# A two-layer graph kernel on one core: complete blocks multiplied once for both layers with 512 columns, and five rounds of early sums for the first tiles

## The reference

```
# layer 0
deg = sum(adj, axis=1);  x1 = adj @ x / deg
x = layernorm(x + concat([x1, x]) @ weight + bias)
# layer 1
h = x @ W.T;  e = h@a1 (row) + h@a2 (column), -inf where adj == 0
x = layernorm(x + softmax(e, axis=1) @ h)
```

## Time and profile before

| | us |
|---|---|
| three runs: lowest, median, highest | 1010.03, 1012.83, 1012.96 |
| the profiled execution, its own time | 1011.9 |
| its span in the profile | 1010.2 |
| PE busy | 970.8 (96%) |
| DVE busy | 732.5 (73%) |
| ACT busy | 601.8 (60%) |
| first pass (tiles 0 to 63) ends at about | 750 |

### The profile page before, as it was taken

The page is one execution under the profiler, slowest core; times in us unless marked ns, Lnnn a source line. Parts: engine busy times, 40 slices in busy tenths (PEclk is TensorE's granted clock), DMA queues, the critical chain, the costliest instruction groups (busy, mean ns, idle before and its releaser), DMA issues.

```text
span 1010.2 us, 22065 instructions
## 1 busy us (share of the span) xinstructions
PE 970.8 (96%) x8727; PEld 866.9 (86%) x8727; DVE 732.5 (73%) x1791; ACT 601.8 (60%) x604; POOL 277.1 (27%) x275
## 2 busy tenths in 40 slices
PE   6899889999999998999999999999999999999996
PEld 6899767888988897888898888888888888888885
DVE  3698887888877786778777676666654986677674
ACT  3988898888878887988868676767421000000000
POOL 4345544333435433434333333332000000000000
PEclk9999989999998999999999999999999999999999
DMA  9999999999999999999999999999421022222101
GB/s 283 394 420 420 421 420 421 419 421 421 421 421 417 420 418 422 415 419 414 410 392 362 420 344 349 341 350 311 159 77 71 22 84 86 90 90 89 34 24 34
DMA packets 50490, 301.70 MB, mean 299 GB/s; under 512 B 6608, under 2 KB 7888, under 8 KB 17360
## 3 DMA queue, kind: packets, MB, share of 16 engines
q0 software_dynamic: 37344, 270.03, 66.9%
q1 hardware_dynamic: 12336, 29.47, 8.7%
q10 hardware_dynamic: 704, 0.75, 0.3%
HBM read 286.46 MB, written 13.76 MB: 297 GB/s over the span
## 4 chain that ended last, share of the span: by engine, by line
PE 61%; DMA 27%; ACT 7%; issue 3%; DVE 2%; POOL 0%; ACTq 0%; DVEq 0%
PE ps_agg L403 33%; DMA adj_in<-in_adj_dram,chunk 26%; PE ps_part L403 22%; ACT edges L585 5%; PE ps_y L403 4%; PE ps_h L752 1%; ACT parts L576 1%; PE ps_h L707 0%; DMA x_all<-in_x_dram 0%; DVE parts L911 0%; PE ps_x1T L745 0%; POOL adj_in L1399 0%; DVE packed L963 0%; DVE edgesT L948 0%; PE ps_y L707 0%
## 5 line engine op out<-in xcount | busy, mean ns | idle before, releaser
L403 PE MATMUL ps_agg<-parts,edgesT 128*128 128x255 f16 (+1 forms) x5240 | 592.3, 274 | 20.3 <-DVE edgesT L948 18.9
L403 PEld LDWEIGHTS ps_agg<-parts,edgesT 128*128 128x128 fp8e4 x5240 | 514.2, 98 | 85.7 <-DVE edgesT L948 24.2
L585 ACT ACTIVATE edges<-adj_in 128x2048 fp8e4<-128x2048 int32 x256 | 481.2, 1905 | 62.8 <-DMA adj_in<-in_adj_dram,chunk 61.2
L1399 POOL DMA_INDIRECT adj_in<-in_adj_dram,chunk x256 | 272.2, 1063 | 430.4 <-ACT edges L585 419.7
L948 DVE STREAM_TRANSPOSE edgesT<-edges 128x512 uint32<-128x512 uint32 x256 | 167.1, 691 | 60.2 <-ACT edges L585 59.6
L403 PE MATMUL ps_part<-parts,edgesT 128*128 128x256 f16 x1664 | 190.2, 273 | 0.3 <-DVE parts L1050 0.3
L403 PEld LDWEIGHTS ps_part<-parts,edgesT 128*128 128x128 fp8e4 x1664 | 162.8, 98 | 18.8 <-DVE parts L1050 0.5
L652 ACT ACTIVATE std<-mean_var,eps 128x1 f32<-128x1 f32 x64 | 18.9, 295 | 226.4 <-DVE mean_var L1224 226.4
L963 DVE SCALAR_TENSOR_TENSOR packed<-edgesT,packed 128x2048 uint32<-128x2048 uint32 x48 | 109.6, 2283 | 1.2 <-DVE packed L959 0.5
L403 PE MATMUL ps_part<-parts,packed 128*128 128x256 f16 x772 | 87.2, 273 | 0.0
L403 PEld LDWEIGHTS ps_part<-parts,packed 128*128 128x128 fp8e4 x772 | 75.6, 98 | 8.7
(11 more groups left out here) (125 smaller groups left out, 655.3 us busy)
## 6 DMA issues: line engine op xcount, KB each, us to landing
adj_in<-in_adj_dram,chunk POOLq DMA_INDIRECT x256
adj_in<-partial_sums SPq DMA_DIRECT2D x16, 256.0 KB, 5.7
out_dram<-edges SPq DMA_DIRECT2D x60, 64.0 KB, 3.3
partial_sums<-partial SPq DMA_DIRECT2D x13, 256.0 KB
packed_adj<-parts SPq DMA_DIRECT2D x2, 1024.0 KB
adj_in<-packed_adj SPq DMA_DIRECT2D x2, 832.0 KB, 5.1
x_all<-in_x_dram POOLq DMA_DIRECT2D x6, 256.0 KB, 13.1
x_all<-in_x_dram SPq DMA_DIRECT2D x6, 256.0 KB, 14.8
```

The source lines that it names most:

```text
L403: done = eng.matmul(bank[:, 0:cols], rows[:, n // BYTES, n % BYTES, :], moving[:, n, :], start=(n == first), stop=(n == last))
L585: act.activation(edges[:, r // 2, r % 2, :], adj_in[:, m % SLOTS, :], ACT.Copy, scale=EDGE[t % GROUP], saturate=False).then_inc(s_conv, 1)
L1399: pool.indirect_dma_start(adj_in[:, m % SLOTS, :], None, adj_chunks, bass.IndirectOffsetOnAxis(chunk[:, 0:1], 0), element_offset=first_row ...
```

## The change

- `parts0` and `parts1` become one tile `rows01`, in which a block has 512 fp16 columns: 256 of the first layer, then 256 of the second.
- For tiles of group g >= 3, `first_layer(t)` issues block 0 with all 512 columns, then the blocks that are not complete (from `done` = 4(g - 1) on) with 255. `hidden(t - 3)` follows, and then `both_layers(t)`: it waits for `s_lo1 >= g - 1` and issues blocks 1 to done - 1 with 512 columns. Both sums lie in the one bank `ps_agg[t % 2]`; `s_agg` is raised at the end of `both_layers`, so that `degree(t)` and `keep_partial(t)` both wait for that. `ps_part` is no longer used in the first pass.
- The caught tiles come in five rounds, two tiles at a time in four of them: groups 0 and 1 get 4 groups of blocks, group 2 gets 3 (before 2, 3 and 4). That is 176 matmuls, 32 more than before, and 32 fewer behind the first pass. Their sums alternate between two banks, and two more stores go to `part_dram`; the loads of these and two additions on DVE come behind the first pass.
- Words and sums that lie in late blocks are now strided by block, so the stores of these (`store_caught`, and `store_words` of pairs 0 and 1) have runs of 512 B in place of 2 KB and 8 KB. The stores of pairs 1 and 0 come one group later.

```diff
-    CATCH = 12
-    CAUGHT = [2, 3, 4]
+    ROUNDS = [(0, 0, 2, 12, 2), (1, 0, 2, 14, 2), (2, 0, 3, 16, 1), (0, 2, 2, 20, 2), (1, 2, 2, 22, 2)]
...
-        parts0 = sb("parts0", [P, NBLK, 2 * F], fp16)
-        parts1 = sb("parts1", [P, NBLK, XCOLS], fp16)
+        rows01 = sb("rows01", [P, NBLK * BOTH + 2 * NBLK], fp16)
+        both = rows01[:, 0:NBLK * BOTH].rearrange("p (n f) -> p n f", f=BOTH)
+        parts0 = both[:, :, 0:2 * F]
+        parts1 = both[:, :, 2 * F:BOTH]
...
             for g in range(GROUPS - 1):
+                for k in range(len(ROUNDS)):
+                    if GROUP * g < kept_at(k) < GROUP * (g + 1):
+                        store_caught(k)
...
-                    if g == KEEP_UNTIL[n] - 1:
+                    if g == KEEP_UNTIL[n]:
                         store_words(n)
...
+            def bank_ready(t):
                 pe.wait_ge(s_tr, NQ * (t + 1))
                 wait(pe, s_z, t - 1)
+                if inline(t - 2):
+                    pe.wait_ge(s_partk, t - 2 - EARLY + 1)
...
+            def first_layer(t):
+                words, done = by_bands(edgesT[:, t % 2, :]), GROUP * bands_of(t // GROUP)
+                bank_ready(t)
+                if not inline(t):
...
+                else:
+                    contract(pe, ps_agg[t % 2], words, both, [0], 0, done - 1)
+                    contract(pe, ps_agg[t % 2], words, parts0[:, :, 0:LO + KEPT_F], range(done, NBLK), 0, done - 1)
+
+            def both_layers(t):
+                done = GROUP * bands_of(t // GROUP)
+                pe.wait_ge(s_lo1, bands_of(t // GROUP))
+                contract(pe, ps_agg[t % 2], by_bands(edgesT[:, t % 2, :]), both, range(1, done), 0, done - 1)\
+                    .then_inc(s_agg, 1)
...
-            def second_layer_inline(t):
...
-                pe.wait_ge(s_lo1, bands)
-                wait(pe, s_partk, t - EARLY)
-                contract(pe, ps_part, edgesT[:, t % 2, :], weighted_rows, range(0, bands * GROUP), 0, bands * GROUP - 1)\
-                    .then_inc(s_part, 1)
...
             def keep_partial(t):
                 g, c = t // GROUP, t % GROUP
-                dve.wait_ge(s_part, t - EARLY + 1)
+                dve.wait_ge(s_agg, t + 1)
...
-                if catching(t):
-                    unpack_caught(t - CATCH)
-                if catching(t - 1):
-                    keep_caught(t - 1 - CATCH)
                 if t // GROUP in odd_groups and t % GROUP == GROUP - 1:
                     check(t // GROUP, 0)
...
                 if joins:
                     check(t // GROUP - 1, 1)
                     join(t // (2 * GROUP) - 1)
+                for i, k, c in caught_at(t):
+                    unpack_caught(i, k, c)
+                for i, k, c in caught_at(t - 1):
+                    keep_caught(i, k)
...
+                for i, k in enumerate(SECOND):
+                    if c == 0 and g == ROUNDS[k][0]:
+                        dve.wait_ge(s_partld2[i], 16)
+                        dve.tensor_tensor(part_in[:, s, :], part_in[:, s, :], part_in[:, 5 + i, :], ALU.add)\
+                            .then_inc(s_pjoin, 1)
```

More of the change, by code:

```diff
@@ L53, in bass_two_graph_layers, with caught_at @@
     EARLY = FIRST_INLINE * GROUP
-    CATCH = 12
-    CAUGHT = [2, 3, 4]
-    CTILES = GROUP * len(CAUGHT)
-    CWORDS = P * max(CAUGHT)
+    ROUNDS = [(0, 0, 2, 12, 2), (1, 0, 2, 14, 2), (2, 0, 3, 16, 1), (0, 2, 2, 20, 2), (1, 2, 2, 22, 2)]
+    CAUGHT = [max(first + bands for g, first, bands, at, by in ROUNDS if g == k) for k in range(FIRST_INLINE)]
+    CBANDS = max(bands for g, first, bands, at, by in ROUNDS)
+    SECOND = [k for k in range(len(ROUNDS)) if ROUNDS[k][1] > 0]
+    def caught_at(t):
+        return [(GROUP * k + c, k, c) for k, (g, first, bands, at, by) in enumerate(ROUNDS) for c in range(GROUP)
+                if t == at + c // by]
     def bands_of(g):
@@ L328, in bass_two_graph_layers @@
         s_partld = [sem(f"partial_landed{s}") for s in range(5)]
+        s_partld2 = [sem(f"partial_of_second_round_landed{g}") for g in range(len(SECOND))]
+        s_pjoin = sem("rounds_added")
         s_unp = sem("unpacked")
@@ L383, in on, with round_home @@
             return 0 <= t - lag < TILES
[L385 to L386 removed]
+        def round_home(k):
+            return GROUPS + SECOND.index(k) if k in SECOND else ROUNDS[k][0]
         def inline(t):
@@ L752, in hidden, with caught @@
                 pe.matmul(ps_h[:, 0:HCOLS], x1T[:, :], w1_cols[:, :], start=True, stop=True).then_inc(s_h, 1)
[L754 to L764 removed]
+            def caught(i, k):
+                g, first, bands, at, by = ROUNDS[k]
+                blocks = range(GROUP * bands)
                 if i == 0:
@@ L767, in caught @@
                 pe.wait_ge(s_cunp, i + 1)
-                wait(pe, s_ckept, i)
-                contract(pe, ps_caught, c_words[:, i % 2, :], weighted_rows, range(blocks), 0, blocks - 1).then_inc(s_csum, 1)
+                wait(pe, s_ckept, i - 1)
+                contract(pe, ps_caught[i % 2], c_words[i % 2], weighted_rows[:, GROUP * first:NBLK, :],
+                         blocks, 0, blocks[-1]).then_inc(s_csum, 1)
             def second_layer(u, blocks):
                 first = GROUP * done_of(turns[u] // GROUP)
-                last = contract(pe, sums[u % 4], words_of_turn[u % 4], weighted_rows, blocks, first, NBLK - 1)
+                last = contract(pe, sums[u % 4], by_bands(words_of_turn[u % 4]), weighted_rows, blocks, first, NBLK - 1)
                 if blocks[-1] == NBLK - 1:
```

108 lines of the change are left out of this document (54 added, 54 removed).

## The result

| | us |
|---|---|
| kernel before, four runs beside it: lowest, median, highest | 1009.64, 1011.43, 1012.96 |
| changed kernel, four runs: lowest, median, highest | 1067.24, 1069.82, 1073.47 |
| ratio, with its 95% interval | 1.057 (1.0547 to 1.0593) |
| changed kernel, profiled execution, its span | 1067.56, 1065.4 |

The change makes the kernel 5.7% slower. 1063 was forecast.

The account below looks back on a forecast made before the run. Loads were taken to bound the kernel up to tile 35, then PE. On 1011.9 us, +10 +32.3 +12 -3.1 +2.6 -3.5 gave 1062.2; with 0.9 for the median, 1063, range 1042 to 1078 for 8 in 10.

Parts of the forecast that it names:

- The new wait: Every fourth tile, PE waits for DVE's weighted_lo with few matmuls as cover: +32.3 us from tile 36, bounds 27 and 36.
- The clock: Tiles 40 to 60: PE's clock drops behind six waits, 2.0 us each, +12 us, bounds 0 and 18.
- A wide matmul: On PE, one merged matmul of 512 columns takes 215.8 ns against 218.4 for two narrow ones.
- The gain of -3.1: From tile 36 on, merging 1232 pairs of matmuls on PE saves 3.1 us; bounds 0 and -3.1.
- rival 3: A wide matmul costs as little as 109.2 ns, -131 us on PE; rather 960 to 1000 us; chance 0.04.
- Before tile 36: DVE waits for slow 512 B stores of caught sums, with smaller waits: tile 36 starts 10 us late, bounds +1 and +14.
- rival 1: Small packets flow, so DVE's four waits on the stores are absent, all else stays: 1054 us; chance 0.21.
- End of the first pass: Tile 63's chain starts with PE's end, so x1 comes later and PE idles: +2.6 us.
- The caught matmuls: 32 more matmuls move from behind the first pass into tiles 12 to 15, where PE waits for loads: -3.5 us.
- Rival 4: Clock stays low through the tile behind each wait, and the stores reach their upper bound: 1078 us; chance 0.09.

Follow-up runs that it names:

- Experiment 1: Changed kernel with the wait on weighted_lo cut in two, so only the last four wide matmuls wait for the new group: 1020.64 us, ratio 1.0073.
- experiment 5: Kernel before, nothing merged, with PE waiting for the newest weighted_lo ahead of the 64 narrow matmuls from tile 36 on: 1060.24 us, ratio 1.0479.
- Experiment 6: Changed kernel with 224 extra matmuls put in ahead of the wait on weighted_lo in tiles 36 to 60: 1053.90 us, ratio 1.0419.
- experiment 8: Changed kernel with split wait, one-piece caught sums, pair 1's words stored a group earlier, 22 second-layer matmuls ahead of h(62): 1008.40 us, ratio 0.9967.
- experiment 2: Changed kernel with the caught sums in a buffer of their own, one piece of 2 KB a partition instead of four of 512 B: 1054.97 us, ratio 1.0409.
- experiment 3: Changed kernel with one-piece caught sums and the kernel before's three rounds of caught tiles instead of five: 1055.66 us, ratio 1.0417.
- experiment 4: Changed kernel with both the wait on weighted_lo cut in two and the caught sums in one piece of 2 KB: 1012.05 us, ratio 0.9995.
- experiment 7: Changed kernel with two buffers for the caught sums, used in turn, a copy waiting for the store of two rounds earlier: 1053.85 us, ratio 1.0419.

## Why the prediction was right, step by step

- **The new wait** (32.3 us from tile 36 on): 31.1 measured, 1.8, 4.8, 4.9, 5.4, 5.7, 4.1 and 4.4 us where 2.1, 4.9, 5.1, 5.5, 6.0, 3.9 and 4.7 were forecast (tiles 36, 40, ... 60); with 0.17 us more for each, 32.2. Experiment 1 gives the cover back and the waits go; experiment 5 makes the waits in a kernel without any merge. The two halves of the mechanism, few matmuls in front and DVE's chain wholly behind PE's end, can be read in the tile-60 rows.
- **The clock** (+12): the tiles from 36 to 63 lost 41.3 us, the waits are 31.1 and merging gives -2.9 to -3.1, so about 13.2. Of that, 1.2 are the seven times 0.17, and 12.1 are slow matmuls: set against 215.8 ns each, those behind the waits of tiles 40 to 60 take 2.3, 2.1, 2.7, 1.9, 1.4 and 1.7 us longer, those of tile 36 no longer at all. Experiment 6 took just 12.1 away with the waits' ends in place, and experiment 5 has 11.8 of it without a wide matmul. The 2.0 us per wait was a size taken over from waits half as long; that it fits on the average was in part luck, as a longer wait did not cost more.
- **A wide matmul** at 215.8 ns: 215.9. The gain of -3.1: -2.9 in experiment 8. With this, rival 3 falls. The sustained 131 ns at N=512 of the Trainium skill ("TensorE: Matmul & The Clock Gate", "Back-to-back issue gap") does not hold here; the 216 ns that the same section gives for an isolated matmul is what this stream of them measured.
- **Before tile 36** (+10, bounds +1 and +14): this is the term that was mis-sized. From tile 12 to 36 the kernel lost 15.0 us, outside the bounds. The miss stood at tile 26, with 17.3 us lost in place of 12.1; from there to tile 36 2.3 came back, where 2.2 were forecast. The landing after 14.5 us was right (14.3 to 14.7, and 16.4 for the fourth), and with it one packet for one, and rival 1 falls. The 9 to 17 descriptors in a row of the Trainium skill ("DMA: Bandwidth & Descriptors", "Queues, rings and completion order") do not show here: each small packet is followed by a load. The prediction's working from that page was unsound, though. It set runs of small packets against single loads; were the loads drained in runs as well, a store would take as long as one for one. What failed is when the copies came due: 9.1, 11.2, 10.4 and 9.4 us after the issue, where the waits that I had worked out imply 10.3, 10.8, 12.6 and 11.5. So DVE waited 19.9 us, not 12.8: 5.1 of the 7.1 more by the earlier copies, 2.0 by the landings, nearly all of it the fourth. Stores alone left tile 36 at +8.3 (experiment 1). The waits in tiles 24, 28 and 32, of together 5.3 us, added as much to that (13.5 against 8.3), where I had 4.4 for the last two. Tile 20 had no such wait. With the stores mended, those same waits cost nothing by tile 36 (experiment 2). That they are hidden there by loads which bound the kernel, and no longer once it is late, fits the traces; it was not tried apart.
- **End of the first pass** (+2.6): 2.1 (56.9 - 54.8). I had reckoned with x1(63); PE waited for h(62), 2.36 us, as ACT's copy of x1(62) stands in its list behind the square root for tile 63, which now comes later. The amount was about right, the place one tile off.
- **The caught matmuls** (-3.5): from x1(63) to the end the changed kernel gained 1.6. The 3.5 are there (experiments 2 and 3 differ by just that behind x1(63)). Of the 1.9 that went again, the slow clock has a part: behind the wait for h(62) eight matmuls take 1.91 us in place of 1.04. In experiments 4 and 6 they take 1.04, and these gain 2.8 and 3.1. The other 1 us or so was not looked for.
- **Rival 4** (the clock stays low for the whole tile) falls by the stretch at 1.00 above; its upper bound for the stores, +14, was nearer than my +10.

The sum came to 1062.2 for an execution that took 1067.56: 5.0 of the difference is the term before tile 36, the rest small ones (+1.9 behind the pass, -0.5 at its end, -1.5 by the early start, +0.5 outside the span). The median of the runs, 1069.82, lies 2.3 above that execution, where 0.9 was added.

## What to carry to other kernels

Before two loops over the same blocks are merged, look at what the first one hid: its matmuls here were the cover under which another engine finished the second one's operand. If only the last few blocks wait for the newest operand, the merged loop covers that wait as the two loops did: here nothing of it was left from tile 36 on. A merge that saves only instructions (2.5 ns of 218) is worth 0.3%, 2.9 us here, and a single wait of tiles 40 to 60 with the slow clock behind it costs 5.7 us or more. And where a layout is changed, its stores' piece sizes change too: ask for each of them who waits for its landing.

## What the runs showed of the hardware

- A store of 0.26 MB beside full loads landed after 7.0 us in packets of 2 KB and after 14.4 in packets of 512 B; one of 1 MB in packets of 512 B took 45.9 us. The small packets went one at a time between loads of 8 KB, and a kernel with small packets and nobody waiting for them was no slower than one without (experiments 7 and 2).
- Behind waits of 4.1 to 5.7 us on PE in tiles 40 to 60 the wide matmuls took 1.4 to 2.7 us longer, with a granted clock of 0.50 in the two stretches shown; behind one of 1.84 us it was 1.00. Filled with matmuls down to about 1 us, they cost none of it. But the length of the wait alone does not decide: 3.56 us in experiment 5 were followed by 1.00, and 2.93 us in the kernel before by 0.50. What does is left open by these runs.
